# A two-layer graph network on one core: lookups of the placing stage in bf16 with its running table kept by VectorE, and a wait for the DMA four back at each indirect DMA

## What is computed

```
# layer 0: attention over edges, 8 heads of 16
q, k, v = x @ Wq.T + bq, x @ Wk.T + bk, x @ Wv.T + bv
scores  = sum(q[src] * k[dst], -1) / sqrt(16) + edge_attr_8
w       = exp(scores) / segment_sum(exp(scores), src)[src]
x       = layernorm(x + segment_sum(v[src] * w, dst) @ Wo.T + bo)
# layer 1: an MLP on each edge, summed at its source, and an MLP on each node
h       = silu(concat(x[src], x[dst], edge_attr_2) @ eW1 + eb1)
e       = silu(h @ eW2 + eb2)
x       = layernorm(x + silu(concat(x, segment_sum(e, src)) @ nW1 + nb1) @ nW2 + nb2)
```

## Time and profile before

| | us |
|---|---|
| runs, median of 3 | 6323.74 (6316.65 to 6324.87) |
| profiled execution, its time | 6342.63 |
| its span | 6340.9 |
| its mean TensorE clock | 0.702 of full |

### The profile page before, as it was taken

The page is one execution under the profiler, slowest core; times in us unless marked ns, Lnnn a source line. Parts: engine busy times, 40 slices in busy tenths (PEclk is TensorE's granted clock), DMA queues, the critical chain, the costliest instruction groups (busy, mean ns, idle before and its releaser), DMA issues. The chain is left out here.

```text
span 6340.9 us, 92597 instructions
## 1 busy us (share of the span) xinstructions
PE 4009.8 (63%) x25409; PEld 3210.9 (51%) x25410; DVE 2375.7 (37%) x6465; ACT 1209.7 (19%) x2122; POOL 3666.3 (58%) x3321
## 2 busy tenths in 40 slices
PE   6899999993333334322666556666346777777776
PEld 4555565562222222212555555555226677667764
DVE  6344434442222222257333333333253433433334
ACT  0222222220111111101111111111122333333332
POOL 0456655555666666632888888888305555555551
PEclk9975555555656556656777777777567888888888
DMA  2100000002111111111444444443411111111111
GB/s 109 58 10 10 10 10 10 10 10 68 43 42 43 43 43 41 43 26 12 36 36 35 36 36 35 36 36 35 109 50 39 37 38 38 37 37 37 36 37 51
DMA packets 278674, 238.37 MB, mean 38 GB/s; under 512 B 57254, under 2 KB 246758, under 8 KB 278245
## 3 DMA queue, kind: packets, MB, share of 16 engines
q0 software_dynamic: 198144, 170.19, 17.3%
q1 hardware_dynamic: 77604, 54.50, 2.8%
q10 hardware_dynamic: 2880, 13.11, 0.5%
HBM read 143.89 MB, written 93.71 MB: 37 GB/s over the span
## 5 line engine op out<-in xcount | busy, mean ns | idle before, releaser
L1060 POOL DMA_INDIRECT sums_dram<-we_merged_rows,we_idx x832 | 1286.1, 1546 | 427.7 <-issue 202.2
L1687 POOL DMA_INDIRECT ed_bg<-b_rows_dram,ed_idx x832 | 792.5, 952 | 676.1 <-DVE ed_idx L1695 458.2
L652 POOL DMA_INDIRECT records_dram<-rec_out,row_idx x784 | 768.6, 980 | 566.5 <-issue 284.7
L751 POOL DMA_INDIRECT sc_k<-k_rows_dram,sc_idx x832 | 802.4, 964 | 470.7 <-issue 249.9
L1212 PE MATMUL ps_merged<-we_rows,we_same_dst 128*128 128x129 f32 x1664 | 355.4, 380 | 588.4 <-issue 435.6
L1212 PEld LDWEIGHTS ps_merged<-we_rows,we_same_dst 128*128 128x128 f32 x1664 | 304.2, 273 | 623.2 <-issue 613.3
L853 PE MATMUL ps_q<-tab,sc_oht 128*128 x2496 | 361.5, 264 | 348.6 <-issue 345.0
L1832 PE MATMUL ps_ed_s<-ed_ohf,ed_efs 128*128 128x128 f32 x1664 | 433.8, 417 | 215.5 <-ACT ed_efs L1772 149.0
L853 PEld LDWEIGHTS ps_q<-tab,sc_oht 128*128 128x128 bf16 x2496 | 250.2, 104 | 458.2 <-issue 404.0
L779 DVE TENSOR_TENSOR sc_prods<-ps_q,sc_k 128x1024 f32<-128x1024 f32 x104 | 127.1, 1222 | 933.0 <-remote 911.0
L1832 PEld LDWEIGHTS ps_ed_s<-ed_ohf,ed_efs 128*128 128x128 f32 x1664 | 339.0, 232 | 258.7 <-issue 217.0
(11 more groups left out here) (288 smaller groups left out, 7889.4 us busy)
## 6 DMA issues: line engine op xcount, KB each, us to landing
sc_k<-k_rows_dram,sc_idx POOLq DMA_INDIRECT x832
sums_dram<-we_merged_rows,we_idx POOLq DMA_INDIRECT x832
ed_bg<-b_rows_dram,ed_idx POOLq DMA_INDIRECT x832
sums_dram<-zero_rows ACTq DMA_DIRECT2D x20, 640.0 KB, 8.5
records_dram<-rec_out,row_idx POOLq DMA_INDIRECT x784
co_rows<-sums_dram SPq DMA_DIRECT2D x48, 256.0 KB, 3.9
records_dram<-rfill SPq DMA_DIRECT2D x16, 416.0 KB, 6.9
records<-records_dram SPq DMA_DIRECT2D x1, 6656.0 KB, 18.8
```

What stands on the lines that cost most here:

```text
L652: pool.indirect_dma_start(c.rec_rows, bass.IndirectOffsetOnAxis(ap=idx[:, b, j:j + 1], axis=0), out[:, b, j, :], None, bounds_check=SLOTS ...
L751: pool.indirect_dma_start(kg[:, r, k * F:(k + 1) * F], None, c.k_dram[:, :], bass.IndirectOffsetOnAxis(ap=idx[:, r, k:k + 1], axis=0)).the ...
L1060: pool.indirect_dma_start(c.acc_dram[k][:, :], bass.IndirectOffsetOnAxis(ap=idx[:, r, k:k + 1], axis=0), rows[:, r, k, 0:F], None, compute ...
L1687: pool.indirect_dma_start(bg[:, r, k * F:(k + 1) * F], None, c.b_dram[:, :], bass.IndirectOffsetOnAxis(ap=idx[:, r, k:k + 1], axis=0)).the ...
```

## The change

It has two parts that touch different instructions.

**Lanes.** `LANES = 4`. In placing, scoring and edges each indirect DMA k now adds to the semaphore k mod 4. Before it, POOL waits until all earlier DMAs on that semaphore have landed, which is the one four back, and adds one to a semaphore nobody waits for. The readers (DVE L779 and L1710, and the writer of `row_idx`) wait on all four. `weigh` is not changed.

**Placing.** The running table no longer goes through PE. `count` starts its PSUM tile with the first of the 8 matmuls; DVE, not ACT, takes it (`keep`): a copy of 50 columns, a sum of 400 columns from PSUM with the last running table, a cast of 400 columns to bf16 and a subtraction of 400 columns for a second bf16 part. `slots_of` looks up with two bf16 matmuls, one for each part, in place of one in float32. ACT's float32 copy of the turned one-hot is gone, and the bf16 one is doubled. `place_ohw` is now laid out tile by tile with its 50 windows next to each other. The bias matmul is bf16 with three rows, which DVE prepares once. PE does `count` and `gram` ahead of `slots_of`; DVE does `nodes`, `keep`, `earlier`, `finish`, with `windows` inside `finish`.

```
+LANES = 4
@@ placing, VectorE
+                def keep(i, b):
+                    g = 2 * i + b
                     wait_count(dve, s_slots, g - 1)
+                    dve.wait_ge(s_hist, g + 1)
+                    wait_count(dve, s_tab, 2 * g)
+                    before = e.start[:, :] if isinstance(g, int) and g == 0 else kept[:, 1 - b, PG, :]
+                    dve.tensor_copy(kept[:, b, 0, :], before).then_inc(s_tab, 1)
+                    dve.tensor_tensor(kept[:, b, 1:PG + 1, :], pstab[:, 0:PG * WC].rearrange("p (k w) -> p k w", w=WC),
+                                      before.unsqueeze(1).to_broadcast([P, PG, WC]), ALU.add).then_inc(s_tab, 1)
+                    dve.wait_ge(s_tab, 2 * g + 2)
+                    dve.tensor_copy(kb[:, b, 0], kept[:, b, 0:PG, :]).then_inc(s_parts, 1)
+                    dve.wait_ge(s_parts, 2 * g + 1)
+                    dve.tensor_tensor(kb[:, b, 1], kept[:, b, 0:PG, :], kb[:, b, 0], ALU.subtract).then_inc(s_parts, 1)
...
-                    wait_count(dve, s_sent[b], 16 * PG * i)
+                    for n in range(LANES):
+                        wait_count(dve, s_sent[n], 16 * (PG // LANES) * (g - 1))
...
-                    for by, work in ((1, earlier), (2, nodes), (0, finish), (2, windows)):
+                    for by, work in ((2, nodes), (1, keep), (1, earlier), (0, finish)):
@@ placing, ScalarE
-                    act.activation(lt[:, :, :].rearrange("p k n -> p (k n)"), pst[:, :], ACT.Copy).then_inc(s_lt, 1)
-                    act.activation(ltf[:, b].rearrange("p k n -> p (k n)"), pst[:, :], ACT.Copy).then_inc(s_lt, 1)
+                    act.activation(lt[:, b].rearrange("p k n -> p (k n)"), pst[:, :], ACT.Copy).then_inc(s_lt, 1)
@@ placing, TensorE
-                    pe.matmul(psx[:, 0:3 * F], one[:, :], bias[:, :], start=True, stop=False)
+                    pe.matmul(psx[:, 0:3 * F], c.ones[:, :], bk[:, :], start=True, stop=False)
...
-                    pe.matmul(table, c.ident[:, :], before.unsqueeze(1).to_broadcast([P, PG + 1, WC]),
-                              start=True, stop=True)
                     for k in range(PG):
-                        ins = pe.matmul(table[:, k + 1:PG + 1, :], ohl[:, b, :, k],
-                                        ohw[:, b, :, k].unsqueeze(1).to_broadcast([P, PG - k, WC]),
-                                        start=False, stop=True, skip_group_check=True)
+                        ins = pe.matmul(table[:, k:PG, :], ohl[:, b, :, k],
+                                        ohw[:, b, k, :].unsqueeze(1).to_broadcast([P, PG - k, WC]),
+                                        start=(k == 0), stop=True, skip_group_check=True)
...
-                        pe.matmul(slots[b][:, k, :], ltf[:, b, k, :], kept[:, b, k, :], start=True, stop=False)
-                        ins = pe.matmul(slots[b][:, k, :], gm[:, b, k, :], ohw[:, b, :, k], start=False, stop=True)
+                        for j in range(2):
+                            pe.matmul(slots[b][:, k, :], lt[:, b, k, :], kb[:, b, j, k, :], start=(j == 0), stop=False)
+                        ins = pe.matmul(slots[b][:, k, :], gm[:, b, k, :], ohw[:, b, k, :], start=False, stop=True)
@@ placing, GpSimd (scoring and edges have the same lines, with s_k and s_b, s_began, and no bounds)
+                        n = j % LANES
+                        wait_count(pool, s_sent[n], 16 * ((PG // LANES) * g + j // LANES))
+                        pool.sem_inc(s_free, 1)
                         pool.indirect_dma_start(
...
-                            out[:, b, j, :], None, bounds_check=SLOTS - 1, oob_is_err=False).then_inc(s_sent[b], 16)
+                            out[:, b, j, :], None, bounds_check=SLOTS - 1, oob_is_err=False).then_inc(s_sent[n], 16)
@@ scoring, VectorE (edges alike)
-                    dve.wait_ge(s_k[r], ring_count(g, r, 16 * SG))
+                    for n in range(LANES):
+                        dve.wait_ge(s_k[n], 16 * (SG // LANES) * (g + 1))
```

More of the change, by code:

```diff
@@ L401, in place_and_project @@
         w = sb("w_qkv", [P, 3 * F], F32)
[L402 to L403 removed]
+        bias = sb("b_qkv", [P, 3 * F], F32)
+        bp = sb("b_qkv_parts", [P, 3, 3 * F], BF16)
+        bk = sb("b_qkv_rows", [P, 3 * F], BF16)
         xt = sb("xt", [P, P], F32)
@@ L486, in finish @@
                     dve.wait_ge(s_slots, g + 1)
-                    dve.tensor_tensor(own[:, :, :], slots[b], ohw[:, b].rearrange("p w k -> p k w"), ALU.mult).then_inc(s_msk, 1)
+                    dve.tensor_tensor(own[:, :, :], slots[b], ohw[:, b], ALU.mult).then_inc(s_msk, 1)
+                    dve.wait_ge(s_msk, g + 1)
+                    ahead, half, there = pair_at(i, b, 2)
+                    if there:
+                        windows(ahead, half)
                     if win is not None:
                         part(win, 0)
-                    dve.wait_ge(s_msk, g + 1)
                     dve.tensor_reduce(slot[:, :], own[:, :, :], AX_X, ALU.add).then_inc(s_red, 1)
@@ L527, in step, with bias_rows_of_qkv @@
                             work(at, half)
+                    if isinstance(i, int) and i == -1:
+                        windows(0, b)
+                    if isinstance(i, int) and i == -1 and b == 1:
+                        bias_rows_of_qkv()
+                def bias_rows_of_qkv():
+                    dve.wait_ge(s_w, 96)
+                    n = 0
+                    for j in range(3):
+                        dve.tensor_copy(bp[:, j, :], bias[:, :]).then_inc(s_bias, 1)
+                        n += 1
+                        dve.wait_ge(s_bias, n)
+                        if j < 2:
+                            dve.tensor_tensor(bias[:, :], bias[:, :], bp[:, j, :], ALU.subtract).then_inc(s_bias, 1)
+                            n += 1
+                            dve.wait_ge(s_bias, n)
+                    dve.tensor_scalar(bk[:, :], bp[:, 0, :], c.ident[:, 0:1], None, ALU.mult).then_inc(s_bias, 1)
+                    for j in (1, 2):
+                        n += 1
+                        dve.wait_ge(s_bias, n)
+                        dve.scalar_tensor_tensor(out=bk[:, :], in0=bp[:, j, :], scalar=c.ident[:, j:j + 1],
+                                                 in1=bk[:, :], op0=ALU.mult, op1=ALU.add).then_inc(s_bias, 1)
                 each_pair(dve, step, lead=1)
@@ L560, in step @@
                 def step(i, b):
-                    ahead, half, there = pair_at(i, b, 1)
-                    if there:
-                        keep(ahead, half)
                     if b == 0 and (not isinstance(i, int) or 0 <= i < NW):
@@ L1707, in summed @@
                     dve.wait_ge(s_z, g + 1)
-                    dve.wait_ge(s_b[r], ring_count(g, r, 16 * G))
+                    for n in range(LANES):
+                        dve.wait_ge(s_b[n], 16 * (g + 1))
                     wait_count(dve, s_htr, g - 1)
```

69 lines of the change are left out of this document (33 added, 36 removed).

## The result

| | before, us | after, us | ratio (95%) |
|---|---|---|---|
| runs, first session | 6323.01 (4 runs) | 6436.57 (4 runs, 6435.59 to 6441.28) | 1.0183 (1.0165 to 1.0201) |
| `after_again` | 6352.67 | 6514.45 | 1.0253 (1.0229 to 1.0278) |
| `after_c` | 6355.73 | 6516.34 | 1.0254 (1.0237 to 1.0272) |

The change makes the kernel slower by 1.8 to 2.5%. I had forecast 4.3% faster. The profiled execution has a span of 6439.6 us, 98.7 above that of before.

What follows compares the result with a forecast made beforehand. Placing was held by PE, scoring and edges by late TensorE signals during gathers. Placing's net 273 us off 6342.6 gave 6070; runs lie 18.9 us lower, so 6050 (chance 0.53), 8-in-10 range 5500 to 6110.

Steps and rivals of the forecast that it cites:

- So POOL becomes the bound, and placing goes from 13.14 to 10.3: 97 x 2.84 = 275 us: Placing: POOL's 8 x 1.285 = 10.28 us a group exceeds PE's 9 and VectorE's 7.2 to 8.3, saving 275 us.
- What scoring and edges share against the other two is that they gather: Scoring and edges: gathers, not the missing wait, mark the stages with late TensorE signals; they keep 12.33 and 7.09 us.
- The hold-up: Scoring and edges: TensorE's signals come late while gathers run, so the pace is a run of gathers and a pause.
- -273 us: Placing's forecast net gain: 275 us, less the part of the bias preparation not under the start's waits.
- cost 0: Placing, scoring, edges: POOL's added wait for the DMA four back costs 0, with 1.3 us of slack.
- the wait blocks in the gather stages: Rival, scoring and edges: landing signals come late and POOL stops after each four; 324 us lost, 6374; chance 0.05.
- Does the wait end the hold-up? I take no.: Scoring and edges: the added wait leaves late TensorE signals as they are; stages keep 12.33 and 7.09 us a group.
- The first rival: Scoring, edges: the wait ends the hold-up in one or both; both 5529 us, one alone 5761 to 5818; chance 0.32.
- The sizes in placing: Placing, per group: PE 8.0 to 9.9 us, taken as 9; VectorE 7.2 to 8.3, with `keep` 1.77; POOL 10.28.
- placing gets less: Rival, placing: PE or the ring of waits through VectorE stays above POOL; 11.5 us a group, 6166 us; chance 0.10.
- that I gave 0.04: Placing: scatters' descriptors wait while VectorE works on SBUF alone, up to 1.23 us a group, 6171 us; chance 0.04.

Runs made afterwards that it cites:

- after_again: The kernel after, unchanged, run again on the chip of the clean session beside the kernel before; 6514.45 us against 6352.67, ratio 1.0253.
- after_c: The kernel after, unchanged, once more in a further session beside the kernel before; 6516.34 us against 6355.73, ratio 1.0254.
- placing_only_b: The kernel after without lanes (also placing_only): 6327.35 us, 1.0016 of the kernel before; in the clean session, as placing_only, 5463.58 us, 0.9614.
- the clean session: One session of a chip, without late TensorE signals in the four kernels traced; the kernel before took 5681.83 us there, 6320 to 6360 in all others.
- lanes_only: The kernel before with the lanes and their waits, placing otherwise unchanged; 5688.98 us (1.001) in the clean session, 6408.1 us (1.0144) in another.

## Why the prediction was wrong

**What failed** is the step "So POOL becomes the bound, and placing goes from 13.14 to 10.3: 97 x 2.84 = 275 us", and under it the sentence "What scoring and edges share against the other two is that they gather". The hold-up does not belong to gathers. It comes with runs of indirect DMAs, scatters too, that start up to 1.46 us apart, and did not come at 1.68. Placing's scatters stood 1.28 us apart before too, but TensorE held the stage back and gave POOL a pause after each eight; the earlier trace rows shows that idle time, 446.2 us, and I read it as slack to be won. With it four in five of TensorE's signals fell into the pause or beside the first six scatters of a run, where none of 188 was late. With the work taken off TensorE most runs became 16 scatters long (16 to 32 in `placing_only_b`), and of the signals raised beside the fifth scatter or a later one 125 of 134 came late, many of them only after the run. POOL then ran out of indices, so it was not the bound. In the place of -273 us stand +76 with the lanes, and 0.2% for the placing change alone.

**The lanes "cost 0".** Right in what it looked at: in the trace of the kernel after the waits held POOL up inside a group in fewer than ten of 832 cases in either gather stage, the 0.30 us between DMAs stayed, and in the clean session the price is 0.1%. Wrong as a sum: 1.4% where signals are late, about half of it from increments. The rival "the wait blocks in the gather stages" gave the right sign by a mechanism that did not happen.

**"Does the wait end the hold-up? I take no."** Right: 162 late signals of 253 in scoring, as before, and 12.34 us a group. The first rival fell.

**The sizes in placing.** `keep` was forecast at 1.77 us and takes 1.67 (808.31 to 809.98). The count takes 1.54 us (804.04 to 805.58; forecast 1.8 to 3.2), 24 lookups 1.04 (827.30 to 828.34) where I had 3.1. TensorE was over-priced, so the error was not there. In the clean session, where POOL's pace could show, `placing_only` stood at 10.90 and not at 10.3, from 13.16 in `lanes_only`: 97 x 2.26 = 219 us, four fifths of the 273. POOL was the bound as forecast, but its scatters had grown (groups of `placing_only`, 300 to 1200 us, as in the earlier trace rows):

```profile
L684 POOL DMA_INDIRECT records_dram<-rec_out,row_idx x649 | 695.4, 1071 | 206.0 <-issue 193.5 <-DVE rec_out L544 12.5
```

With the mean over the whole stage, 1.066 us, it is 8 x (1.066 + 0.304) = 10.96 us a group. 271 of the 784 scatters took over 1.05 us, and of those that lay beside `keep`'s cast or subtraction on VectorE 91 and 97% did; they were 1 to 2% of the short ones. So the part of the rival "placing gets less" that I gave 0.04 has the right size in this one run: 8 x (1.066 - 0.981) = 0.68 us a group, 66 us. The rule of the Trainium skill, "SBUF — State Buffer", section "SBUF: two separate sides", that GpSimd can't write descriptors while VectorE's copies hold the port they share, fits this, though the node one-hot, a comparison, lies beside long scatters too (65% of those beside it). But lying beside VectorE's work is not enough: in the kernel after in its own session the mean stayed 0.980 us (768.2 for 784), as before, and of the 94 scatters beside the cast 4 were long, of the 101 beside the subtraction 9. What else it takes is open.

What was only argued: that runs of DMAs and TensorE's signals share a path that backs up. The runs show when the signals are late and what changes it, not what the path is, nor why the clean session had none of it with runs of 112 scatters.

## What to carry to other kernels

An engine's idle time can be what keeps another engine's signals on time; before counting it as gain, look at what the stage does where that idle time is missing, and here showed it two stages later. A kernel that issues many indirect DMAs should be compared beside its predecessor in more than one session: the same placing change was 3.9% faster in one and 0.2% slower in another. Where consumers wait for "remote" long after TensorE's matmul ended, try a short pause on GpSimd ahead of each group before taking any more work off TensorE; it does not make late signals rare, but it bounds how long they are late.

## What the runs showed of the hardware

TensorE's signals can arrive 25 us after the matmul that raises them, while GpSimd issues indirect DMAs 1.25 to 1.46 us apart. It takes a run of them: in scoring 0 of 60 signals beside the first two gathers of a run were late and all 150 from the fourth on. In the placing of the kernel after 101 of the 171 late ones came only after the run's last scatter had ended, half of those by 2.7 us or less, and the other 70 while it lasted. TensorE's own issue slows down in the meantime: in the kernel before it started a weight load or a matmul at 2004.57, 2005.97, 2007.37, 2008.07, 2009.47, 2010.17 and 2010.88 us, so every 0.7 or 1.4 us, and waited for nothing that the trace shows. At 1.68 and 1.85 us apart none of 254 and 746 was late, and twice as many matmuls did not change this at 1.85 (none of 698). Placing's scatters took 1.07 us on the mean and not 0.98 in `placing_only`, where 87 of the 96 beside VectorE's cast were long; in the kernel after it was 4 of 94. And in one session nothing of the late signals was to be seen: the same kernel before ran in 5682 us and not in 6320.
